# First edge sum of a graph network: gathered rows land in four places of their own, and ScalarE copies them into a ring of 52

## The reference, cut to what matters

```python
h = jnp.einsum('nd,df->nf', x, W)                       # first layer only
agg = jax.ops.segment_sum(edge_weight[:, None] * h[src], dst, num_segments=6250)
```

## Time and profile before

| what | value |
|---|---|
| median of 3 runs | 3900.63 us (3893.59 to 3905.37) |
| span of the profiled execution | 3891.6 us |
| profiled execution's own time | the profile gives none beside its span; the median of the runs is 9.0 us above the span |
| mean granted TensorE clock | 0.819 |
| busy: TensorE, VectorE, GpSimd, ScalarE | 68%, 66%, 56%, 26% |
| first edge sum | 369.8 us (first gather) to 1558 us |
| second edge sum | gathers from 1952 to 3110 us |

### The profile page before, as it was taken

One profiled execution on the slowest core, in us unless ns is written; L12 is line 12 of the kernel. 1 busy time (PEld: TensorE's weight loads), 2 busy tenths in 40 slices (PEclk: granted clock), 3 DMA queues, 4 the chain that ended last, 5 costly groups with the idle time before them and its releaser, 6 DMA issues. The chain is left out here.

```text
span 3891.6 us, 55224 instructions
## 1 busy us (share of the span) xinstructions
PE 2650.3 (68%) x15016; PEld 2238.8 (58%) x15016; DVE 2586.9 (66%) x6599; ACT 1024.1 (26%) x2120; POOL 2179.1 (56%) x2145
## 2 busy tenths in 40 slices
PE   6886555444454545789946666666666657999998
PEld 4666343333343434689935444444444537999998
DVE  8997655444554555976746566666666677888886
ACT  0021000000000000567501111111111127888886
POOL 1434566666666664335456666666666603666665
PEclk8998777777777777899967777777887768999999
DMA  3011333333333332000133333333333334776775
GB/s 90 4 46 58 102 91 92 91 91 88 91 92 88 92 88 63 12 1 23 55 90 96 96 96 96 96 96 94 98 95 94 95 103 165 216 216 212 213 215 146
DMA packets 164219, 387.69 MB, mean 100 GB/s; under 512 B 46324, under 2 KB 95528, under 8 KB 150561
## 3 DMA queue, kind: packets, MB, share of 16 engines
q0 software_dynamic: 99072, 233.49, 22.0%
q1 hardware_dynamic: 64929, 151.65, 11.4%
HBM read 342.69 MB, written 42.97 MB: 99 GB/s over the span
## 5 line engine op out<-in xcount | busy, mean ns | idle before, releaser
L1089 POOL DMA_INDIRECT g_got<-table,e_source x1568 | 1493.5, 952 | 845.0 <-issue 440.0
L1115 DVE TENSOR_TENSOR A<-A,psum 128x256 f32 x1664 | 698.6, 420 | 876.3 <-remote 532.0
L1182 PE MATMUL psum<-g_got,g_route 128*128 x3328 | 1034.7, 473 | 141.0 <-DMA g_got<-table,e_source 74.2
L1182 PEld LDWEIGHTS psum<-g_got,g_route 128*128 128x128 f32 x3328 | 771.9, 241 | 329.0 <-issue 198.4
L786 PE MATMUL psum<-ident,g_rows 128*128 128x128 f32 x208 | 63.0, 401 | 663.3 <-ACT A L834 410.2
L1098 DVE TENSOR_SCALAR g_route<-columns,e_local,e_weight 128x128 f32<-128x128 f32 x1664 | 471.6, 362 | 17.4 <-issue 12.2
L786 PEld LDWEIGHTS psum<-ident,g_rows 128*128 128x128 f32 x208 | 29.7, 190 | 703.8 <-ACT A L834 505.7
L834 ACT COPY A<-psum 128x256 f32 x52 | 19.3, 372 | 999.4 <-issue 637.4
L369 POOL DMA_INDIRECT records<-rec,place x120 | 120.6, 1005 | 233.7 <-ACT rec L585 159.1
L140 PE MATMUL psum<-e_xt_hi,e_w_hi 128*128 128x256 f32 x832 | 238.2, 286 | 5.4 <-issue 5.2
L1612 POOL TENSOR_TENSOR f_ht_lo<-f_ht,f_ht_hi 128x512 fp32r<-128x512 f32 x100 | 134.2, 1347 | 181.1 <-ACT f_ht_hi L1551 174.6
(11 more groups left out here) (413 smaller groups left out, 5403.5 us busy)
## 6 DMA issues: line engine op xcount, KB each, us to landing
e_w<-in_m_w SPq DMA_DIRECT2D x104, 1024.0 KB, 5.1
g_got<-table,e_source POOLq DMA_INDIRECT x1568
expert_table<-g_normal SPq DMA_DIRECT2D x52, 128.0 KB
table<-xn SPq DMA_DIRECT2D x49, 128.0 KB
X<-in_x SPq DMA_DIRECT2D x1, 6144.0 KB
table<-f_ring SPq DMA_DIRECT2D x24, 256.0 KB, 2.1
out<-X SPq DMA_DIRECT2D x1, 6144.0 KB
f_w<-in_f_w SPq DMA_DIRECT2D x2, 1024.0 KB, 6.5
```

Of the source, the lines that this page charges most:

```text
L1089: pool.indirect_dma_start(got[:, c % RING, :], None, rows, bass.IndirectOffsetOnAxis(ap=source[:, c:c + 1].bitcast(U32), axis=0)).then_inc ...
L1115: dve.tensor_tensor(to, to, sums_of(c), ALU.add).then_inc(added, 1)
L1182: ins = pe.matmul(sums_of(c), route[:, c % (GB + GSEM), :], row(got, at[j % GSEM]), start=True, stop=True)
```

## The change

In the first edge sum only, gathers no longer land in the ring. GpSimd waits until a landing place is free (`copied`), issues a pair of gathers into `landing` (4 places, `LAND`), and counts each pair on one of the eight semaphores. ScalarE waits for a pair, and for the old chunk's last slot where a ring place is used again, and copies chunk by chunk from `landing` into `got`. TensorE waits for `copied` instead of the gather semaphores. ScalarE's work for the finished tiles is put between the copies: it copies for slots up to 4 (`AHEAD`) past the group after the one named, and `keep_across` of a tile moves from its own step into the next. The ring has 52 places instead of 56 in both edge sums, and the second sum's waits for its gathers start from a constant 1568.

```diff
-RING = 56
+RING = 52
+LAND = 4
+AHEAD = 4
...
+                landing = None if through_mlp else here("landing", [P, LAND, D])
+                copied = None if through_mlp else sem("g0_copied")
...
-                    earlier = -(-(CHUNKS // GSEM - q % 8) // 8) if through_mlp else 0
-                    return (earlier + q // 8 + 1) * (16 * GSEM)
+                    return CHUNKS // 8 * 16 + (q // 8 + 1) * (16 * GSEM)
+
+                def chunk_bound(slot):
+
+                    return min(CHUNKS - 1, (GB * slot + GB - 1) // (GB + 1))
...
-                    for q in range(CHUNKS // GSEM):
-                        if not through_mlp and q * GSEM in (0, 4 * P):
-                            pool.wait_ge(edges.sources_made, 1 + (q > 0))
+                    for pair in range(0 if through_mlp else CHUNKS // 2):
+                        if 2 * pair in (0, 4 * P):
+                            pool.wait_ge(edges.sources_made, 1 + (pair > 0))
+                        wait(pool, copied, 2 * pair + 2 - LAND)
+                        pool.sem_inc(dma_open, 1)
+                        for c in range(2 * pair, 2 * pair + 2):
+                            pool.indirect_dma_start(
+                                landing[:, c % LAND, :], None, rows,
+                                bass.IndirectOffsetOnAxis(ap=source[:, c:c + 1].bitcast(U32), axis=0)
+                            ).then_inc(gathered[pair % 8], 16)
+                    for q in range(CHUNKS // GSEM if through_mlp else 0):
...
+                            else:
+                                pe.wait_ge(copied, chunk_bound(first + GSEM - 1) + 1)
...
-                    for n in range(1, STEPS):
+                    copies = [0]
+
+                    def copy_rows(slot):
+
+                        for c in range(copies[0], chunk_bound(slot) + 1):
+                            if c % 2 == 0:
+                                act.wait_ge(gathered[c // 2 % 8], (c // 16 + 1) * 32)
+                            if c >= RING:
+                                wait(act, pairs_summed, (c - RING + NT - 1) // 2 + 1)
+                            act.copy(got[:, c % RING, :], landing[:, c % LAND, :]).then_inc(copied, 1)
+                        copies[0] = chunk_bound(slot) + 1
+
+                    before_tile = None
+                    for n in range(0 if through_mlp else STEPS):
+                        copy_rows(n * GB + GSEM - 1 + AHEAD)
+                        if n >= 2:
+                            tiles_of.keep_across(act, n - 2, before_tile)
+                        copy_rows(n * GB + 2 * GSEM - 1 + AHEAD)
+                        if n >= 1:
+                            act.wait_ge(added, n * GB + 1)
+                            before_tile = tile_to_finish(n, mybir.EngineType.Activation)
+                            tiles_of.tile.stage(act, n - 1, before_tile)
+                        copy_rows(n * GB + 3 * GSEM - 1 + AHEAD)
+                        if n >= 1:
+                            tiles_of.keep_turned(act, n - 1)
+                        copy_rows(n * GB + 4 * GSEM - 1 + AHEAD)
+                    if not through_mlp:
+                        tiles_of.keep_across(act, FINISHES - 1, before_tile)
```

More of the change, by code:

```diff
@@ L53 @@
 assert MIN_PAIRS > PEELED and (MTILES - 2 * MIN_PAIRS) * MT % (2 * P) == 0
-assert EP * EJ == E and NG * GC == EJ and RUNS_D * RUN * P < BIG and CHUNKS % GSEM == 0 and SLOTS % GB == 0 and RING % GSEM == 0 and NT % GROUP == 0 and GROUPS % 2 == 1
+assert EP * EJ == E and NG * GC == EJ and RUNS_D * RUN * P < BIG and CHUNKS % GSEM == 0 and SLOTS % GB == 0 and RING % GSEM == 0 and LAND == GSEM and CHUNKS // 2 % 8 == 0 and NT % GROUP == 0 and GROUPS % 2 == 1
 LN_EPS = 1e-5
@@ L1171, in _ @@
                             first = n * GB + g * GSEM
-                            for q in range(asked[0], landed_by(first) + 1):
-                                pe.wait_ge(gathered[q % 8], gathered_after(q))
-                            asked[0] = landed_by(first) + 1
+                            if through_mlp:
+                                for q in range(asked[0], landed_by(first) + 1):
+                                    pe.wait_ge(gathered[q % 8], gathered_after(q))
+                                asked[0] = landed_by(first) + 1
+                            else:
+                                pe.wait_ge(copied, chunk_bound(first + GSEM - 1) + 1)
                             _, at = nc.values_load_multi_w_load_instructions(
@@ L1214, in _ @@
                         act.wait_ge(tiles_of.loaded, tiles_of.LOADS * 16)
-                    for n in range(1, STEPS):
+                    copies = [0]
[23 more added lines that the diff above has]
+                        tiles_of.keep_across(act, FINISHES - 1, before_tile)
+                    for n in range(1, STEPS if through_mlp else 1):
                         act.wait_ge(added, n * GB + 1)
@@ L1231, in _ @@
                                 tiles_of.keep_normal_turned(act, n - 3)
-                        else:
-                            tiles_of.keep_turned(act, n - 1)
-                            tiles_of.keep_across(act, n - 1, t)
                     if through_mlp:
```

## The result

| | before | after |
|---|---|---|
| median of 4 runs each | 3900.01 us | 3951.77 us |
| ratio, with its 95% interval | | 1.0134 [1.0111, 1.0157] |
| span of the profiled execution | 3891.6 us | 3946.4 us |
| mean granted clock of TensorE | 0.819 | 0.810 |
| first edge sum, first to last gather | 1150.8 us | 1202.5 us |

The kernel became 1.3% slower (the interval lies above 1), where 6.8% was forecast.

A forecast was written before the change was run, and what follows sets the result against it. The prediction took TensorE's late completion signals during streaming gathers to bound the first edge sum. Span 3891.6 us plus 260 (longer steps) and 5 (ring) gave 4157, plus 9 to the runs' median scale: about 4165, range 3770 to 4230.

The forecast's parts named there:

- What bounds the kernel: First edge sum: TensorE's completion signals come late while gathers stream, mostly not before the stream stops; GpSimd pauses 3.6 us a step.
- lateness begins after some 8 us of stream: First edge sum: TensorE's signals come late once gathers have streamed for more than some 8 us.
- If the signal stays late, a step becomes: First edge sum: 15.1 gathers, then 8.6 us pause; 27.4 to 28.8 us a step, +260 us taken; chance 0.50.
- rival (a): First edge sum: gaps before pairs let signals through, stage runs at GpSimd's pace; -113 us, 3788; chance 0.30.
- rival (b): First edge sum: signal late in only part of the steps, by timing after GpSimd's restart; about 4035 us; chance 0.14.
- The pace: First edge sum: landing loop gives a gather every 1.25 to 1.34 us, 1.30 taken.
- copies signalled late (1.40): Faster case, first edge sum: late `copied` signals slow gathers to 1.40 us each; 3835 us.
- The copies: First edge sum: 784 SBUF copies on ScalarE, 315 us of work, covered because ScalarE is nearly idle.
- The ring of 52: Second edge sum: gathers wait for a slot four later; between nothing and 25 us, 5 taken.
- (c): First edge sum: signal some 8 us late without waiting for the stream's end, no net change; 3900 us; chance 0.06.

The follow-up runs named there:

- z_single: Changed kernel with gathers issued and copied one by one instead of in pairs, late chip, one run: 4051.68 us, kernel before 3919.71.
- z_land6: Changed kernel with six landing places instead of four, gathers still in pairs, late chip: 4019.85 us, 1.025 against the kernel before.
- v_half: Kernel before with first-sum gathers of 512-byte rows (half the bytes, as many gathers), late chip, one run: 3964.75 us, kernel before 3939.84.
- v_ring52: Kernel before with a ring of 52 places instead of 56, late chip, one run: 3957.68 us, kernel before 3939.84.
- z_gap448: Kernel before with a 448-column memset behind each pair of first-sum gathers, late chip, one run: 3892.48 us, kernel before 3919.71.
- y_single: Changed kernel with gathers issued and copied one by one instead of in pairs, prompt chip: 3548.97 us, 1.0121 against the kernel before.
- z runs: Three kernels on one late chip (single gathers, six landing places, 448-column gaps): 4051.68, 4019.85 and 3892.48 us, kernel before 3919.71.
- y_after: The changed kernel itself, unchanged, on a prompt chip: 3678.89 us, 1.0486 against the kernel before.

## Why the prediction was right and wrong

**What bounds the kernel: right on this chip.** VectorE's nameless wait for TensorE, with GpSimd's pause behind it, is there wherever a late chip runs an unbroken stream of gathers (z_single, z_land6, v_half, v_ring52, every second sum), and it is gone where the stream has gaps of 1.23 us. On prompt chips it isn't there at all, and the kernel before takes 10% less. The premise that lateness begins after some 8 us of stream does not hold for streams with short gaps: in the kernel after no more than four gathers, some 5 us, follow one another without a distance of 1.31 us or more, and adds are still late by up to 9.8 us. That the signal is what is late is still an inference from start times; no run here shows the signal itself.

**The step that failed: "If the signal stays late, a step becomes" 15.1 gathers "and then a pause" of 8.6 us, in each of 46 steps.** Two things were wrong in it.

- *How often.* The landing loop does not issue gathers in an unbroken stream. z_single and z_land6 close the stream, with the landing, the ring and the copies kept, and 49 and 52 long pauses appear, 292 and 283 us (31 and 17 of them in one pause at the sum's start, where the kernel before has one of 16). The change has 20, 91 us, and 22 late steps of 52 where they have 49. Gaps alone, put into the kernel before, also make the long pauses rare (z_gap448, 12, 29 us), though they leave 33 steps late by less. So with the change's own slow loop more than half of the steps escape. That is the mechanism of rival (a), working part of the time, with rival (b)'s pattern (4035), though (b) had placed the escape in the timing after GpSimd's restart and not in the gaps. I had written that nothing in the trace showed a stream with such gaps; that was the place to widen (b)'s chance beyond 0.14.
- *How long.* Where the pause comes in every step (z_single) it is mostly 6.4 to 6.6 us, not 8.6, and the step 25.0 us, not 27.4 to 28.8. In the step shown the first two adds of the group are already let go at 1009.15, while gathers are issued. From the start of the late add to the end of ScalarE's copy into A it is 2.5 us instead of 4.0, and from there to GpSimd's start 1.1 instead of 1.6. From the last gather's end to the late add it is 3.03 us, as forecast.

In the forecast the pauses were worth 46 x (8.6 - 3.6), or +230 us; they measured -79.

**The pace was mis-sized.** 1.30 us a gather was taken, +39 us over 784. The measured excess of short gaps is 132 us (131 more than before), and on a prompt chip the first sum takes 1.444 us a gather. Part is the loop: a gather's start to ScalarE's copy is 2.76 us instead of 2.5, and GpSimd's start was put at 0.1 to 0.7 and is 0.8, while two copies take 0.71 instead of 0.9, so 1.38 instead of at most 1.34. The rest, some 50 us on the prompt chip, was put at nothing. Part of it is what ScalarE does for the finished tile between the copies (the 5.78 us above); the forecast said that this would hold GpSimd too, but gave it no price. How the 50 us divide isn't shown. Even the rival case's "copies signalled late (1.40)" was short. The two errors, of the pauses and of the pace, have opposite signs: the pauses came out 309 us below their term and the pace 92 above it, together -217. These two terms make 269, where 260 was taken; the first sum's gathers measured +52.

**That it came out slower, as forecast, was luck in the main.** The pauses, which were to make it slower, shrank; it is slower by the pace and the ring, which the forecast had put at 39 and 5 us. The -22 us behind the first sum's last gather had no term.

**The copies** were right as free: y_single is no slower than the ring alone (1.0121 and 1.0127). They measure 283.9 us, 0.72 a pair, where 315 was taken.

**The ring of 52** was put at 5 us, between 0 and 25. The second sum grew by 22.3; on the late chip of the z runs two kernels with 52 places take 1187.2 and 1190.9 us for it and one with 56 takes 1166.9. On the other late chip it is only 7 to 12 us. So the price was mis-sized, and on the result's chip it lies near the upper bound, for the bound's reason as prompt chips show it: a wait of 4.4 to 5.5 us in each of the first four steps that reuse places, where five had been counted. I chose the low end because pauses there seemed to be of the late signal anyway; how far the two overlap on a late chip differs between the two chips. The same price is due in the first sum on prompt chips, which the sum left out; in the changed kernel's first sum on a late chip no run separates it.

**The other rivals.** (a) fell as a whole: 194 us of waits stand in front of gathers. (c), 3900, is the nearest in size, but not by its mechanism: the steps did not stay as they were, they got rarer pauses and dearer gaps.

**No version here beats the kernel before.** z_gap448 is 27 us below it in one run on a late chip, where the kernel before ran from 3912 to 3933 (one run isn't enough for a claim), and the same kernel is 3.9% slower on a prompt one. **Open:** what holds the signals, why on some chips only, how wide a gap is needed (0.65 us shortens the lateness, 1.23 removes it), whether it is the gaps or only the lower rate of gathers (every kernel with gaps has both), and whether the short gaps of the change itself, rather than the pattern of its restarts, decide which steps escape.

## What to carry to other kernels

A wait that ends at nothing the profile names, on an engine whose producer has long finished, can be the cost of an unbroken stream of GpSimd's gathers, as it was here on the late chips; look at whether it starts when the stream stops, and test with gaps and on more than one chip before building around it. If two places are handed back at a time out of four, the loop's period is two starts, a landing, two copies and a signal: here 5.5 us for what should take 5.0, and giving back single places cost nothing and took 130 us off where signals were prompt. A ring's size is paid in the first steps that reuse it, once in each sum: 4 places fewer were 20 us in each on prompt chips.

## What the hardware showed that was not expected

- The same kernel took 3501 to 3509 us on some chips and 3900 to 3940 on others. The two sums' gathers take 986 and 992 us in the trace of a prompt chip and 1151 and 1158 in that of a late one; of the rest of the difference 23 us are the first sum's work behind its last gather (38 and 15) and 26 the stretch behind the second sum (781 and 755). From the end of the first sum's work to the second's first gather both take 393.8 or 393.9 us.
- On a late chip, a sum with 1.23 us between pairs of gathers runs like on a prompt one (1357.6 and 1356.5 us), and half the bytes do not remove the lateness (one long pause a step in v_half).
- Mending the change's loop cost some 80 us on late chips (z_single is 132 us over the kernel before beside it, the change 52 over the one beside it) and gained 130 on a prompt one.
- From the start of a gather of 128 rows of 1 KB to the start of ScalarE's copy that waits for it: 2.76 us in y_after, of which GpSimd holds 0.94.
